# Decoder layer on one core: context keys and a second unit projected ahead of the barrier, second attention's weights in four pieces

## The reference, cut to what matters

```
x = layernorm(x + attn(x))                 # qkv, scores + bias, softmax, o_w
q, k, v = x@Wq+bq, x@Wk+bk, x@Wv+bv        # second attention, self, causal
qc, kc, vc = x@Wcq+bcq, ctx@Wck+bck, ctx@Wcv+bcv
y = softmax(qk)v + softmax(qc kc)vc
x = layernorm(x + y@Wp + bp)
x = layernorm(x + sum_e w_e * gelu(x@Wa[e])@Wb[e])
```

## Time and profile before

| | us |
|---|---|
| median of 3 runs | 1243.82 (1240.8 to 1244.6) |
| the profiled execution | 1243.63 |
| its span, first to last instruction | 1241.9 |
| first attention, up to the barrier | 566.5 |
| TensorE busy | 1167.9 (94%) |
| VectorE busy | 918.6 (74%) |
| ScalarE busy | 820.0 (66%) |
| GpSimd busy | 527.8 (43%) |
| mean granted TensorE clock | 0.979 |

### The profile page before, as it was taken

The page is one execution under the profiler, slowest core; times in us unless marked ns, Lnnn a source line. Parts: engine busy times, 40 slices in busy tenths (PEclk is TensorE's granted clock), DMA queues, the critical chain, the costliest instruction groups (busy, mean ns, idle before and its releaser), DMA issues.

```text
span 1241.9 us, 25141 instructions
## 1 busy us (share of the span) xinstructions
PE 1167.9 (94%) x8869; PEld 528.7 (43%) x8869; DVE 918.6 (74%) x2368; ACT 820.0 (66%) x1577; POOL 527.8 (43%) x530
## 2 busy tenths in 40 slices
PE   6799999999999999978999999899988999999998
PEld 2234434444444444334422333223323366666666
DVE  3567777777777777877888888898886667656564
ACT  4456666666666666654587786787677866666663
POOL 1977778877888888864211212132111140000000
PEclk9799999999999999999999999899999899999999
DMA  6634333423323333204212122112102331423200
GB/s 215 185 90 115 87 99 83 117 82 83 83 83 81 82 83 83 57 1 100 59 46 81 49 65 66 44 50 81 44 27 70 141 132 68 138 84 131 90 18 17
DMA packets 82482, 102.77 MB, mean 83 GB/s; under 512 B 12626, under 2 KB 74066, under 8 KB 82358
## 3 DMA queue, kind: packets, MB, share of 16 engines
q1 hardware_dynamic: 81174, 100.64, 27.6%
q10 hardware_dynamic: 160, 0.39, 0.1%
q0 software_dynamic: 1024, 0.13, 0.1%
HBM read 65.14 MB, written 10.68 MB: 61 GB/s over the span
## 4 chain that ended last, share of the span: by engine, by line
PE 43%; DVE 8%; ACT 2%; issue 2%; ACTq 0%
PE a_s L1420 10%; PE a_m L1406 7%; PE a_o L1339 7%; DVE a_mx L1733 5%; PE a_m L1294 5%; PE a_s L1321 3%; PE a_a L169 3%; PE a_s L1406 2%; PE a_s L169 1%; PE a_m L1300 1%; PE a_a L1364 1%; ACT a_pt L1553 1%; DVE a_r L1745 0%; DVE a_ys L1749 0%; PE a_a L1347 0%
## 5 line engine op out<-in xcount | busy, mean ns | idle before, releaser
L1733 DVE TENSOR_REDUCE a_mx<-a_m 128x1 f32<-128x512 f32 (+3 forms) x512 | 271.8, 583 | 40.8 <-PE a_m L1294 30.2
L1553 ACT ACTIVATE a_pt<-a_s 128x512 f32<-128x512 f32 (+3 forms) x512 | 235.8, 518 | 85.7 <-PE a_s L1321 84.3
L698 ACT ACTIVATE a_pt<-a_s 128x512 f32<-128x512 f32 x256 | 149.5, 597 | 168.0 <-DVE a_s L846 150.5
L837 DVE CUSTOM_DVE_ANT_0 a_junk<-a_m,a_rtile 128x512 f16<-128x512 f32 x256 | 167.3, 687 | 8.2 <-issue 8.2
L942 POOL TENSOR_TENSOR a_ps<-a_ps,a_pt 128x512 f32<-128x512 f32 x126 | 157.7, 1276 | 0.1
L499 PE MATMUL a_o<-a_pt,a_v 128*64 128x512 f32 x512 | 138.1, 617 | 2.6 <-DVE a_a L851 2.5
L1977 POOL TENSOR_SCALAR_AFFINE_SELECT a_pt<-a_pt 128x512 f32<-128x512 f32 x64 | 40.7, 636 | 199.1 <-ACT a_pt L1553 199.1
L846 DVE TENSOR_TENSOR a_s<-a_s,a_near 128x218 f32<-128x218 f32 (+1 forms) x256 | 106.9, 432 | 18.3 <-PE a_s L490 15.9
L826 DVE TENSOR_TENSOR a_nat<-a_a,a_nat 128x512 f16<-128x512 f32 x64 | 44.3, 692 | 90.5 <-ACT a_nat L670 90.5
L489 PE MATMUL a_s<-a_q,a_k 128*128 128x512 f16 x256 | 100.0, 391 | 8.3 <-issue 3.0
L954 POOL TENSOR_TENSOR x_acc<-x_acc,a_part 128x256 f32<-128x256 f32 x120 | 87.4, 728 | 34.6 <-DVE x_acc L869 34.0
(11 more groups left out here) (305 smaller groups left out, 2615.0 us busy)
## 6 DMA issues: line engine op xcount, KB each, us to landing
a_rtile<-lines SPq DMA_DIRECT2D x32, 448.0 KB, 4.0
a_q<-a_nat SPq DMA_DIRECT2D x192, 64.0 KB
a_k<-a_nat SPq DMA_DIRECT2D x192, 64.0 KB
a_vy<-in_Wa SPq DMA_DIRECT2D x12, 1024.0 KB, 4.9
a_vy<-in_Wb SPq DMA_DIRECT2D x12, 1024.0 KB, 7.4
a_qk<-halves SPq DMA_DIRECT2D x40, 128.0 KB, 2.7
halves<-a_held SPq DMA_DIRECT2D x16, 256.0 KB, 2.2
halves<-a_held SPq DMA_DIRECT2D x32, 128.0 KB, 2.4
```

The costliest lines, as they stand in the source:

```text
L698: act.activation(pt[:, n % RING, ::-1], bank_s[j % 2][:, :], ACT.Exp, scale=SC1 / QS).then_inc(sm["act_s"], 1)
L837: dve.tensor_tensor_reduce(junk[h][:, :], bank_m[h][:, :], rtile[:, u % 3, h, qb * P:qb * P + S], -1 / MAXROW, 3e38, ALU.add, ALU.min, mx[ ...
L1553: act.activation(pt[g % 4][:, h, first:], bank_s[(32 * u + j) % 3][:, first:], ACT.Exp, scale=SC2 / QS).then_inc(sm["act_s"], 1)
L1733: dve.tensor_reduce(mx[u % 2][:, qb, to:to + 1], bank_m[j % 3][:, 0:keys], AX.X, ALU.max).then_inc(sm["dve_b"], 1)
```

## The change

- **Weights**: the second attention's weights are loaded and split in four quarters of 640 columns, not in two halves of 1280; ScalarE's parts stand in slots 6, 8, 10 and 12 at i = 1, VectorE's in the same slots at i = 2.
- **Turned copies**: in slots (0, 3), (2, 0) and (3, 0) ScalarE takes them behind the splits of the projection weights and the second exponential, VectorE behind the second bias addition and the maxima.
- **Order of the bridge**: CONTEXT2 at (33, 1), KEYS2 at (33, 3), TURN2 at (34, 2), SELF2 at (34, 3), QUERIES2 at (35, 0), and a new step NEXT2 at (35, 1): TensorE alone projects the self queries and keys of unit 1 into a PSUM bank that both blocks share (m1 of the first, a of the second). The evacuation of that bank (`high_self`, `low_self`) stays behind the barrier; `project_self(1)` there is gone.
- **VectorE's order at (34, 2)**: `invert` of the last unit ahead of the bridge step.
- **Stores and moves**: the cross keys are stored first, with a semaphore of their own. When they have landed, SP loads the constant rows of key buffer 0 ahead of the barrier, and ScalarE issues unit 0's key moves ahead of the barrier, once self's store has landed. Behind it SP waits for the query store alone.
- **Statistics**: three of the last sequence's four bn_stats go to slot 35 (i = 1 to 3), and behind the barrier the memsets follow the statistics.

```diff
-        W2_CUTS = [slice(i * (W2 // 2), (i + 1) * (W2 // 2)) for i in range(2)]
+        W2_CUTS = [slice(i * (W2 // 4), (i + 1) * (W2 // 4)) for i in range(4)]
-        bank_br = [*bank_m, bank_a]
+        bank_br = [*bank_m, *bank_m, bank_a, *bank_m]
-        TURN2, CONTEXT2, SELF2, QUERIES2, KEYS2 = (0, 1), 2, 3, 4, 5
+        CONTEXT2, KEYS2, TURN2, SELF2, QUERIES2, NEXT2 = 0, 1, (2, 3), 4, 5, 6
@@ bridge_at
-            return {(34, 2): TURN2, (34, 3): (CONTEXT2,), (35, 0): (SELF2,), (35, 1): (QUERIES2,), (35, 2): (KEYS2,)}.get((t, i), ())
+            return {(33, 1): (CONTEXT2,), (33, 3): (KEYS2,), (34, 2): TURN2, (34, 3): (SELF2,), (35, 0): (QUERIES2,),
+                    (35, 1): (NEXT2,)}.get((t, i), ())
@@ store_first (SP)
+                sp.wait_ge(second.sm["dve_cross"], 1)
+                store_cross(sp, second, halves2, 1, second.natk, "st_keys")
                 sp.wait_ge(second.sm["dve_self"], 1)
                 store_self(sp, second, halves2, 0)
-                sp.wait_ge(second.sm["dve_cross"], 1)
+                sp.wait_ge(second.sm["st_keys"], 2 * DMA)
+                sp.dma_start(second.k0[3 * D2:P // 2 + 3 * D2 + 1:P // 2, :, :, :].rearrange("p h x s -> p (h x s)"), io["select2"]
+                             ).then_inc(second.sm["cst"], DMA)
+                sp.wait_ge(second.sm["dve_cross"], 2)
                 store_cross(sp, second, halves2, 0, second.natc)
-                sp.wait_ge(second.sm["dve_cross"], 2)
-                store_cross(sp, second, halves2, 1, second.natk)
@@ sync
-                if u == 8:
-                    sp.wait_ge(sm["w2_lo"], 1)
-                    sp.dma_start(w2_raw, io["w2"][:, W2_CUTS[1]]).then_inc(sm["w2_in"], DMA)
+                if u in (6, 8, 10):
+                    n = u // 2 - 2
+                    sp.wait_ge(sm["w2_lo"], n)
+                    sp.dma_start(w2_raw, io["w2"][:, W2_CUTS[n]]).then_inc(sm["w2_in"], DMA)
@@ scalar
-                    b = turned_at(t, i)
-                    if b is not None:
-                        turned.scalar(act, b, b + 1)
...
                     if 0 <= u < UNITS:
                         exponential(u, (i + 3) % 4 * 2 + 1)
+                    b = turned_at(t, i)
+                    if b is not None:
+                        turned.scalar(act, b, b + 1)
...
-                    if t in (6, 10) and i == 1:
-                        split_w2(t // 10)
+                    if t in (6, 8, 10, 12) and i == 1:
+                        split_w2(t // 2 - 3)
...
+            act.wait_ge(second.sm["st_keys"], 2 * DMA)
+            act.wait_ge(second.sm["st_self"], DMA)
+            move_keys(act, second, halves2, 0, second.k0)
@@ vector
-                    b = turned_at(t, i)
-                    if b is not None:
-                        turned.vector(dve, b, b + 1)
...
                     if 0 <= t - 1 < UNITS:
                         maximum(t - 1, i)
+                    b = turned_at(t, i)
+                    if b is not None:
+                        turned.vector(dve, b, b + 1)
+                    if t - 4 == UNITS - 1 and i > 0:
+                        dve.wait_ge(sm["dve_e1"], 4 + i)
+                        norm.statistics(dve, (B - 1) * NT + i - 1)
                     if 0 <= t - 4 < UNITS:
                         add_out(t - 4, i)
-                    if t in (6, 10) and i == 1:
-                        split_w2(t // 10)
+                    if t in (6, 8, 10, 12) and i == 2:
+                        split_w2(t // 2 - 3)
...
-                    for e in bridge_at(t, i):
-                        bridge(e)
                     if (t, i) == (UNITS + 2, 2):
                         invert(UNITS - 1)
+                    for e in bridge_at(t, i):
+                        if e != NEXT2:
+                            bridge(e)
@@ second block: sync, tensor, scalar, vector
-            sp.wait_ge(sm["st_cross"], 4 * DMA)
+            sp.wait_ge(sm["st_cross"], 2 * DMA)
-            for c in range(3):
+            for c in range(1, 3):
-                if u is not None and u > 0 and i % 2 == 0:
+                if u is not None and u > 1 and i % 2 == 0:
                     project_self(u, i // 2)
-            act.wait_ge(sm["st_cross"], 4 * DMA)
-            act.wait_ge(sm["st_self"], DMA)
-            move_keys(act, second, halves2, 0, k[0])
-            dve.memset(bank_o[:, :], 0.0).then_inc(sm["cleared"], 1)
-            dve.memset(ht[RH:RH + 1, :], 1.0).then_inc(rt["one"], 1)
-            for t in range((B - 1) * NT, B * NT):
-                norm.statistics(dve, t)
+            norm.statistics(dve, B * NT - 1)
```

More of the change, by code:

```diff
@@ L155, in __init__ @@
         self.whi, self.wlo = (self.held[:, SPARE + i * W2:SPARE + (i + 1) * W2] for i in range(2))
-        self.sm = semaphores(nc, ctx, "a2", "pe_self act_self dve_self pe_cross act_cross dve_cross st_self st_cross moved")
+        self.sm = semaphores(nc, ctx, "a2", "pe_self act_self dve_self pe_cross act_cross dve_cross st_self st_cross st_keys moved cst")
+        self.bank = ctx.enter_context(nc.psum_tensor("a2_a", [P, 512], F32))
         self.wost = ctx.enter_context(nc.sbuf_tensor("a2_wost", [P, PAIRS, C], F32))
@@ L176, in store_self, with store_cross @@
                  ).then_inc(second.sm["st_self"], DMA)
-def store_cross(sp, second, halves2, c, halves):
+def store_cross(sp, second, halves2, c, halves, stored="st_cross"):
     row = 2 * S
@@ L184, in store_cross @@
         sp.dma_start(bass.AP(halves2.tensor, at, [[row, CG], [P * row, 2], [1, S]]), halves[i * CG:(i + 1) * CG, :, :]
-                     ).then_inc(second.sm["st_cross"], DMA)
+                     ).then_inc(second.sm[stored], DMA)
 def move_queries(engine, second, halves2, u, q):
@@ L255, in attention_1 @@
         bank_a, bank_o = bank("a"), bank("o")
-        bank_s, bank_m, bank_e = ([bank(f"{n}{i}") for i in range(2)] for n in "sme")
+        bank_s, bank_e = ([bank(f"{n}{i}") for i in range(2)] for n in "se")
+        bank_m = [bank("m0"), second.bank]
         scratch = near[:, :, :].rearrange("p h c -> p (h c)")
@@ L553, in bridge @@
             def bridge(e):
-                to = bank_br[e % 3]
-                if e < 2:
+                to = bank_br[e]
+                if e == CONTEXT2:
                     pe.wait_ge(sm["dve_b"], 8 * UNITS)
-                elif e == 2:
+                elif e == SELF2:
                     pe.wait_ge(sm["dve_r"], UNITS)
-                else:
-                    pe.wait_ge(sm["dve_br"], e - 2)
+                elif e == TURN2[1]:
+                    pe.wait_ge(second.sm["dve_cross"], 1)
+                elif e < NEXT2:
+                    pe.wait_ge(sm["dve_br"], 1)
                 if e in TURN2:
@@ L574, in bridge @@
                 else:
-                    pe.wait_ge(sm["dve_br"], TURN2[1] + 1)
-                    at = [QK_AT + c * GROUPS * P if e == SELF2 else CQ_AT + c * C for c in range(KC)]
+                    pe.wait_ge(sm["dve_br"], 3)
+                    at = [CQ_AT + c * C if e == QUERIES2 else QK_AT + (c * GROUPS + e // NEXT2) * P for c in range(KC)]
                     mm = product(pe, to[:, :], [(second.whi[:, o:o + P], second.wlo[:, o:o + P], xhi[:, c, 0:S], xlo[:, c, 0:S])
                                                 for c, o in enumerate(at)])
-                mm.then_inc(sm["pe_br"], 1)
+                mm.then_inc(second.sm["pe_self"] if e == NEXT2 else sm["pe_br"], 1)
             for t in range(SLOTS):
@@ L632, in bridge @@
             def bridge(e):
-                frm = bank_br[e % 3][:, :]
+                frm = bank_br[e][:, :]
                 act.wait_ge(sm["pe_br"], e + 1)
@@ L1040, in attention_2_and_experts @@
         bank_m, bank_s = ([bank(f"{n}{i}") for i in range(3)] for n in "ms")
-        bank_a, bank_o = bank("a"), bank("o")
+        bank_a, bank_o = second.bank, bank("o")
         norm = second.norm
@@ L1536, in high_cross @@
                 if u > 0:
[L1537 removed]
+                    act.wait_ge(sm["st_cross"], 2 * DMA * (u - 1))
                 o = cross_bias(u)
@@ L1704, in vector @@
             norm.variances(dve, B - 1, 1)
+            dve.memset(bank_o[:, :], 0.0).then_inc(sm["cleared"], 1)
+            dve.memset(ht[RH:RH + 1, :], 1.0).then_inc(rt["one"], 1)
             def make(n):
```

12 lines of the change are left out of this document (6 added, 6 removed).

## The result

The changed kernel takes 1246.68 us (median of 20 runs, 1241.78 to 1250.50) against 1243.09 us for the kernel before on the same chip (20 runs): ratio **1.0031, 95% interval 1.0018 to 1.0043**, 3.9 us slower. Measured again on two other chips the ratio was 1.0017 (1.0000 to 1.0034) and 1.0037 (1.0016 to 1.0058). Weighted by their intervals the three give 1.0028, about **3.5 us slower** (2.4 to 4.6). The forecast was 1243.7 us, no change.

A forecast was written before the change was run, and what follows sets the result against it. TensorE was taken as the bound, busy 15.50 of 15.52 us per undisturbed first-attention slot. Terms -0.7 + 0.6 + 2.0 - 1.9 = 0.0 us on 1243.63 us gave 1243.7 us, no change (chance 0.62), range 1239.0 to 1247.8 us.

The forecast's parts named there:

- Weights: Slots 6, 8, 10, 12 of the first attention: four quarters at 1.27 us, 5.1 against 5.79 us for halves, 0.7 us less.
- Rival B: All weight pieces vanish in gaps of the first attention's slots: 1243.7 - 5.1 = 1238.6 us; chance 0.08.
- Turned copies: Ramp of the first attention: slot 2 pays 1.25 us, slot 3 gives part back, +0.6 us in sum.
- First bias addition near 47 us: Sign in slot 2: VectorE's low copies at 45.7 us run ahead of the first bias addition, delaying it 1.25 us.
- Context and keys: Slot 33: waits make the last exponential end 2.75 us later, 0.75 comes back; transposes of x start 2.0 us later.
- The small multiplication: Layer norm, after slot 33: falls from 0.90 to about 0.2 us because GpSimd is idle by then, giving back 0.75 us.
- Table load: Sign after slot 33: the square root's table load starts near 547.7 us, 2.75 us later than 544.92 us.
- Tail: From the transposes of x to the barrier: ends equal within 0.1 us, so the barrier stays +2.0 us, at 568.5 us.
- Behind the barrier: First 8 us behind the barrier: first value copy and first maxima each come 1.9 us sooner, -1.9 us.
- Behind that: Second attention and experts: same instructions in the same order, so a shift goes through to the end; no term.
- rival C: Slower: early keys paid, not given back, +3.9, 1247.6 us; decides if first maxima come over 8 us behind barrier; chance 0.16.
- A: Rival: TensorE's clock stays up in the tail, or in slots 3 and 6: 1243.7 - 4.5 = 1239.2 us; chance 0.14.

## Why the forecast was wrong

**Weights** ("0.7 us less"): the step that failed, by size and by sign. It is +1.6 us, and these 2.3 us are the largest error of the sum. Three errors in it. I charged the halves with a clock fall of 1.45 us in slot 6; of eight profiles with halves at the old place only two have it (17.7 us in the six others), so their price is 4.7, not 5.79. A quarter costs 1.43, not 1.27 us: VectorE's takes 0.88 us where half of 1.57 is 0.79 and I took 0.75. And two slots further on lost 0.28 us each. The mechanism (both pieces pass through) was right: in slot 10 everything is 0.62 us late behind ScalarE's piece and 1.43 us behind VectorE's. That slots 6, 8, 10 and 12 last 1.1 to 1.4 us longer was nearly so. The Trainium skill's warning (Perfetto Trace Analysis, Optimizing Scalar/DVE Operations) that each instruction carries a fixed cost would have made the sum 0.3 us worse; the trace agrees in kind: two quarters take 1.48 and 1.76 us against 1.27 and 1.57 for a half, 0.4 us more per half, 0.8 in all.

**Rival B** (pieces vanish in gaps, 0.08) I turned down with "TensorE's 0.02 us of slack per slot". That argument was false. TensorE's slack says what TensorE may lose; whether a piece on ScalarE or VectorE reaches it depends on whether that engine waits behind the piece, and ScalarE does, 1.3 us in (t, 2). The change's place isn't in a wait, so B didn't happen; but 4 us lay there.

**Turned copies** (+0.6): 1.2 us late in slot 2, as predicted (transfer there at 46.78 us, first bias addition at 49.21, 2.43 us behind it against 1.23), and 0.54 back in slot 3 (15.47 us in all eight profiles, 16.01 at full clock before). That is +0.65; but five of the twelve profiles with the old order also lose 1.45 us of clock in slot 3 and none with the new one does. So the term is near 0; whether the new order keeps the clock up (0 of 8 against 5 of 12) is more than these profiles can show. "First bias addition near 47 us" failed (49.21): see below.

**Context and keys** (+2.0): the wait is 2.76 us at full clock (16.26 to 16.29 in three profiles against 13.51), predicted 2.75. The small multiplication took 0.17 instead of 0.90 us and the transposes came 0.91 sooner, predicted 0.75. What I left out is the clock: in two of the five profiles it fell in these waits, 1.57 us more, 0.6 on average. Table load at 551.45, not 547.7 us: 2.2 us of that were late at slot 33 already.

**Tail**: from the transposes to the barrier's opening 16.5 us on average in the five profiles, 16.6 in the twelve with the old bridge; predicted equal. Self and queries came later than I had worked out (low halves at 563.59 and 566.22, not 558.05 and 562.0 us). Of this 3.6 us had come before, with the transposes at 554.83 instead of 551.2 us; the rest is there because self waited for the low copies of x until 560.12 us; the sums fitted between all the same.

**Behind the barrier** (-1.9): value copy 1.7 and first maxima 2.3 us sooner, as predicted. But VectorE waited for ScalarE's high copy of x at 578.03 us and TensorE 0.94 us for VectorE at 579.99, so at VectorE's next maximum 1.4 us of it were left in this pair of profiles; from the transposes of x to VectorE's first maximum it is 1.6 us on average (24.4 against 26.0).

**Behind that** (nothing in the sum): the prediction says that the same instructions in the same order follow, so that a shift goes through to the end. They took 1.1 us longer by the marks, since the clock fell once more within 44 us of VectorE's first maximum in every profile with the new bridge. This is the second step that failed: 2.3 and 1.1 us are nearly the whole 3.5.

**Rivals and chances.** The sum by marks up to VectorE's first maximum, +2.4 us, is in part what rival C describes: keys paid and only partly given back, weights dearer. Its deciding point didn't come (maxima 6.1 us behind the barrier, under the 8 it named). A did not happen. The time lies in the range, but I gave slower only 0.16: with a sum of 0 made of four terms that cancel, and a clock that falls in some executions and not in others, that was too sure. That the range held is no merit of the sum: it was wide enough for rival C.

## What to carry to other kernels

Work on an engine beside the bottleneck costs by what stands behind it in that engine's order. Look in the trace for the wait that ends last in each part of the loop and put the work ahead of it; here 1.3 us of such a wait took a whole half, and cutting it finer at a place where ready work stood behind it made it worse. A step for three engines in turn should be placed three times, each in its own engine's wait, and not at one point of a common order; here that took 2.1 us out of slot 33, though the measured time doesn't show the gain. Take the price of a clock fall from several executions before it goes into a sum, and look for falls also where no instruction was changed.

## What was not expected of the hardware

The same instructions run at either of two paces in the ramp. The first unit's 24 small matmuls, first in the kernel before, then in the kernel with the weights alone, whose program is the same up to there:

```profile
21.57 0.23 PE L452 MATMUL a_a<-a_whi,xhi 128*128 128x128 f16 x1 [0.47 <-DVE a_nat L826]
21.64 0.22 PE L452 MATMUL a_a<-a_held,xhi 128*128 128x128 f16 x1
```

```profile
22.89 0.29 PE L453 MATMUL a_a<-a_whi,xhi 128*128 128x128 f16 x1 [0.47 <-DVE a_nat L827]
22.97 0.31 PE L453 MATMUL a_a<-a_held,xhi 128*128 128x128 f16 x1
```

They follow each other by 0.05 to 0.06 us in the one and by about 0.11 in the other. That is about the ratio of the two clock levels, but the view by windows has 1.00 as granted clock for both at 22 to 24 us, so that the clock is the cause isn't shown. The start of slot 3 lies between 57.8 and 62.8 us over the 20 profiles, with either order of the turned copies. Later on too: at 616 to 622 us the changed kernel ran at 0.50, the kernel before at 1.00 in the same windows.

```profile
616.00:618.00 2.00, 2.00 (x12) 0.73 (x12) 1.00 (x2) 0.95 (x2) 0.64 (x1) 0.50 0.11 25
618.00:620.00 2.00, 2.00 (x12) 0.50 (x7) 1.85 (x4) 1.53 (x4) 0.00 (x0) 0.50 0.58 170
```

Five of the 20 profiles have this fall, four with the new bridge and one with the old; each loses 2.8 us by it. Five others have the shorter one nearer to the barrier, which costs 1.0 us. TensorE had pauses just before the long one (busy 1.39 and 1.58 us in 612 to 614 and 614 to 616 us), but the profiles without the fall have pauses there too. Differences of 3 us between two single profiles of this kernel say nothing of a change.
